# An attention kernel at its batch boundaries: two normalizing instructions moved behind two copies, and in step 2 two copies moved ahead of two weighings

## The chip, the cores and the metric

The kernel runs on one core of a Trainium2 chip. The metric is the device time of one execution in microseconds (us); lower is better. A core has a matrix engine (PE), a vector engine (DVE), a scalar engine (ACT), a general engine (POOL) and a queue engine that here only issues DMAs (SP). Each works through its own instructions in the order in which they are written; semaphores tie the engines together.

## What is computed

```
x = x + autocorrelation(layernorm(x), ctx, ctx)      # 8 batches, 512 x 2048 each, 8 heads
x = x + ffn(layernorm(x), A_w, B_w, Wq_w, keys)      # 64 experts of rank 8, 16 of them kept

autocorrelation:  corr = ifft(fft(q) * conj(fft(k))).real        # over the 512 positions
                  w, idx = top_k(corr, 12); w = softmax(w)
                  out = sum_i w_i * v[min(idx_i + pos, 511)]
ffn:              gate = softmax over the 16 best of (x Wq^T) keys^T, else 0
                  out  = ((x A^T) * gate) B^T * 2
```

Only the first line, the attention, is touched by the change.

## The kernel before

**Steps.** The attention is cut into 32 groups of 512 columns (`GROUPS`), four to a batch, and runs in 33 steps, written out one after the other. Step `i` has two halves that belong to different groups. For its own group `i` it transforms ctx and x (PE: `ctx_cyclic`, `x_spectrum`, `ctx_negacyclic`), multiplies the spectra (DVE `products`), adds the products (POOL `add_products`, tile `p_f`), goes back to lags (PE `first_corr`, `second_corr`, tile `lag`) and picks the 12 best lags with their softmax weights (DVE `topk`, ACT `big_exp`, `top_exp`, `weigh`). For the group before it, `i - 1`, it finishes the picking of the last two of four tiles, folds the weights (POOL `fold_w`, `fold_edges`), transforms them, multiplies, and turns the result back (PE `out_row`, line L755); `copy_even` (ACT, L1535) and `add_att` (DVE, L1229 and L1230) combine the two halves of that result.

**Names.** `k` is the batch of the step counted from -1, and `r` the quarter: `i = 4k + 3 + r`. A step with `r == 3` (steps 2, 6, 10, ..., 30) computes the normalizers of the next batch. The step after it has `r == 0`; the passage from one to the other is called a boundary here.

**The start of a step on PE.** `ctx_cyclic` makes four products into two PSUM banks in turn (`evac_ps[n % 2]`, line L631). The third and fourth may start only when ACT has copied the first and the second out of their bank. Then PE computes `x_spectrum(0)` (L644), the first product of `ctx_negacyclic` (L655 and L656), `x_spectrum(1)` and three more of the former. The first of the negacyclic products uses the bank of the third cyclic one:

```python
# ctx_cyclic, n = 2 and 3:     pe.wait_ge(evac_act, 6 * i + n - 1)
# ctx_negacyclic, n < 3:       pe.wait_ge(evac_act, 6 * i + 3 + n)
```

So `ctx_negacyclic`'s n = 0 needs three copies of the step done. `x_spectrum(1)` waits for `add_att` of the step before.

**The start of a step on ACT.** First two copies of the cyclic products into `v_cyc` (`evac_from`, L1525), then `last_exponentials`: two exponentials over 512 columns (L1563) and two over 12 (L1567) for group `i - 1`; then the third and the fourth copy, two negated copies (L1529), six one-column instructions (`edges`, L1547 to L1549), and from there the weighing of tiles 2 and 3 (`weigh`, L1540), which wait for DVE, and the copies of the negacyclic products (`v_neg`).

**Normalizing.** `norm` (L1395) scales and shifts a 128 x 512 tile of x, `xf`, in place, four tiles for one group. ACT does it two groups ahead, in one piece behind its `lag_copies` where `r != 3`. In a step with `r == 3` the normalizers come late, and it is done in two halves (`norm_late`): tiles 0 and 1 behind the first `big_exp`, tiles 2 and 3 at the step's end, behind `weigh` of tiles 0 and 1 and ahead of `copy_even`. POOL's `begin_fold_x` (L1775) of the following step reads all four tiles and waits for `normed`; it stands behind `fold_w` of tiles 0 and 1 (L1811 and L1812), and behind it come `middle_fold_x` (L1779), `fold_edges` (L1818, L1819), `fold_w` of tiles 2 and 3, and two `add_products` (L1804) whose `p_f` PE's `first_corr` (L698) needs.

**Step 2** is the first step that weighs tiles 0 and 1 of the group before at its own start instead of at the end of the step before; this stands between the second copy and `last_exponentials`.

Of the kernel before, what the change touches and what calls it, by code (L numbers as in the profile page):

```python
# [16 lines left out]
GROUPS = B * GPB  # L17
LT = L // P
# [115 lines left out]
def build_program(nc, x, ctx, a_w, b_w, wq_w, keys, tables, out):  # L134
# [6 lines left out]
    with ExitStack() as st:  # L141
# [27 lines left out]
        xfs, v_cyc, v_neg = [None, None], [None, None], [None, None]  # L169
# [119 lines left out]
        def is_step(i, n):  # L289
            return isinstance(i, int) and i == n  # L290


        def evac_cyc(i, n):
            return n if is_step(i, 0) else 12 * i - 4 + n

        def evac_neg(i, n):
            return 4 + n if is_step(i, 0) else 12 * i + n
# [16 lines left out]
        def prod_w(i, n):  # L314
            return 6 * i - 2 + n - (2 if is_step(i, GROUPS) else 0)
# [1074 lines left out]
        def _(act):  # L1390
            def norm(k, r, off, tiles, src=None):
                for j in tiles:
                    t = slice(j, j + 1)
                    part = xfs[(3 + r + off) % 2][:, j, :]
                    nc.scalar.activation(part, part if src is None else src[:, j, :], ACT.Identity, bias=shift[:, t], scale=rstd[:, t]).then_inc(normed, 1)  # L1395
# [122 lines left out]
            def body(k, r, a, b, f, s):  # L1518
                i = 4 * k + 3 + r
                cur, before = (r + 1) % 2, r % 2  # L1520


                def evac_from(bank, n, dst):
                    act.wait_ge(evac_ready, n + 1)
                    nc.scalar.activation(dst, evac_ps[bank][:], ACT.Copy).then_inc(evac_act, 1)  # L1525

                def minus(dst, src, n):
                    act.wait_ge(evac_act, n)
                    nc.scalar.activation(dst, src, ACT.Copy, scale=-1.0).then_inc(minus_done, 1)  # L1529
# [7 lines left out]
                def weigh(g, t):  # L1537
                    act.wait_ge(inv_done, CT * g + t + 1)
                    act.wait_ge(picked, CT * g + t + 1)
                    nc.scalar.activation(e[:, t, :], e[:, t, :], ACT.Copy, scale=inv_sum[:, t:t + 1]).then_inc(weighted, 1)  # L1540

                def edges(g, tiles):

                    for t in tiles:
                        act.wait_ge(weighted, CT * g + t + 1)
                        first, second, third, fourth = (e[:, t, n * P:n * P + 1] for n in range(4))
                        nc.scalar.activation(third, third, ACT.Identity, bias=first, scale=-1.0).then_inc(edges_done, 1)  # L1547
                        nc.scalar.activation(pick[:, t, P:P + 1], second, ACT.Identity, bias=fourth).then_inc(edges_done, 1)
                        nc.scalar.activation(pick[:, t, 3 * P:3 * P + 1], fourth, ACT.Identity, bias=second, scale=-1.0).then_inc(edges_done, 1)  # L1549
# [20 lines left out]
                if a:  # L1570
                    if b and not is_step(i, 1):
                        act.wait_ge(prod_ready, prod_w(i - 1, 3) + 1)
                    for part in range(2):
                        evac_from(part, evac_cyc(i, part), v_cyc[cur][:, part, :])
                    if is_step(i, 2):
                        for t in (0, 1):
                            weigh(i - 1, t)
                def last_exponentials():
                    for t in (2, 3):
                        big_exp(i - 1, t)  # L1580
                    for t in (2, 3):
                        top_exp(i - 1, t)
# [1 line left out]
                if b and a and not is_step(i, 1):  # L1584
                    last_exponentials()
                if a:
                    for part in range(2):
                        evac_from(part, evac_cyc(i, 2 + part), v_cyc[cur][:, 3 + part, :])
                    if is_step(i, 1):
                        last_exponentials()  # L1590
                        evac_from(0, evac_neg(i, 0), v_neg[cur][:, 0, :])
                        edges(i - 1, (0, 1))
                    for n in range(2):
                        minus(v_cyc[cur][:, 3 * n + 2, :], v_cyc[cur][:, 3 * n, :], 6 * i + 2 * n + 1)
                        if is_step(i, 1) and n == 0:
                            for t in (2, 3):
                                weigh(i - 1, t)
                    if b and not is_step(i, 1):
                        edges(i - 1, (0, 1))
# [40 lines left out]
                norm_late = i + 2 < GROUPS and r == 3  # L1640
# [23 lines left out]
                if a:  # L1664
# [4 lines left out]
                    if not is_step(i, 1):  # L1669
                        for t in (0, 1):  # L1670
                            weigh(i, t)
                if norm_late:
                    norm(k, r, 2, range(LT // 2, LT))
                if is_step(i, GROUPS - 1):
                    edges(i, (0, 1))
                    copy_even()
# [14 lines left out]
                if is_step(i, GROUPS):  # L1691
                    tile_high(0, 3)
                    tile_root(1)
            steps(body)

            def tile_step(u, k, r, a, b, f):
# [294 lines left out]
```

## Time and profile before

| | |
|---|---|
| time, median of 3 runs | 2156.32 us (2156.14 to 2157.71) |
| the profiled execution's own time | 2156.57 us |
| its span, first to last instruction | 2154.8 us |
| granted TensorE clock over the span | 1.000 |
| PE busy | 2115.7 us (98%) |
| DVE busy | 1673.8 us (78%) |
| POOL busy | 1561.3 us (72%) |
| ACT busy | 1337.5 us (62%) |

The attention takes the span up to about 1310 us, the rest is the feed-forward part. A step of the attention lasts a little over 40 us; the shares of busy time above are averages over both parts. In the rows below, a number in square brackets is the time for which the engine stood idle ahead of that row, with what ended it. A row can stand for several instructions in a run (x2, x4); its length then reaches from the first one's start to the last one's end, and for PE the ends are modelled, so that rows overlap by some 0.17 us.

### The profile page before, as it was taken

To read this page: it belongs to the slowest core of one execution; us is meant where nothing else is said; L and a number is where in the kernel's file an instruction comes from. 1 tells how busy PE (TensorE), PEld (TensorE's weight loads), DVE (VectorE), ACT (ScalarE), POOL (GpSimd) and SP (SyncE) were. 2 spreads that over 40 slices of the span, in tenths; PEclk is the share of its full clock that TensorE was granted. 3 is DMA by queue.
4 is the path that set the end of the run, shared out by engine and by line. 5 is a ranking of instruction groups with operands and counts; after the bars stand their busy time and mean duration, and the time that the engine had idled before them with its cause. 6 is when DMAs were issued, how large, how long until landed. Compare 5 with 4: busy or idle time off the path is not lost.

```text
span 2154.8 us, 29239 instructions
## 1 busy us (share of the span) xinstructions
PE 2115.7 (98%) x8920; PEld 1328.0 (62%) x8920; DVE 1673.8 (78%) x4051; ACT 1337.5 (62%) x3051; POOL 1561.3 (72%) x965
## 2 busy tenths in 40 slices
PE   5999999999999999999999999999999999999999
PEld 2455455455455455454454454888888888888887
DVE  7999999999999999999999999644444444444443
ACT  4786786786786786786765646644444455445441
POOL 6999999999999999999999988633343433333420
PEclk9999999999999999999999999999999999999999
DMA  7232333333333332333221246544545444444431
GB/s 282 97 108 103 120 111 103 120 111 103 121 109 103 121 109 103 122 109 103 103 89 64 83 168 239 171 158 166 175 164 174 159 166 165 158 166 172 164 119 59
DMA packets 110705, 287.50 MB, mean 133 GB/s; under 512 B 7168, under 2 KB 7296, under 8 KB 109568
## 3 DMA queue, kind: packets, MB, share of 16 engines
q1 hardware_dynamic: 110592, 286.19, 38.3%
q8 instruction: 47, 0.77, 0.1%
q14 instruction: 66, 0.54, 0.1%
HBM read 219.06 MB, written 67.11 MB: 133 GB/s over the span
## 4 chain that ended last, share of the span: by engine, by line
PE 82%; DVE 7%; POOL 6%; ACT 2%; issue 2%; DMA 1%; SPq 0%; DVEq 0%; ACTq 0%; POOLq 0%
PE pair L755 11%; PE pair L749 8%; PE out L581 6%; PE out L582 6%; PE out L583 6%; PE z L583 5%; PE z L582 5%; PE z L581 5%; PE pair L644 5%; PE evac L631 4%; PE evac L655 4%; PE evac L656 4%; PE lag L698 4%; PE pair L745 4%; PE tp L600 2%; POOL r_f L1804 2%
## 5 line engine op out<-in xcount | busy, mean ns | idle before, releaser
L1838 POOL TENSOR_TENSOR rows<-rows,cin 128x1024 f32<-128x1024 f32 x48 | 117.0, 2437 | 325.7 <-DMA rows<-out_dram 273.6
L755 PE MATMUL pair<-r_f,back 128*128 128x512 f32 x768 | 342.7, 597 | 0.5 <-DVE prod L1035 0.5
L1804 POOL TENSOR_TENSOR r_f<-prod 128x1024 f32<-128x1024 f32 x128 | 303.0, 2378 | 9.3 <-DVE prod L1033 7.4
L755 PEld LDWEIGHTS pair<-r_f,back 128*128 128x128 f32 x768 | 143.0, 190 | 192.7 <-issue 146.5
L749 PE MATMUL pair<-w_sb,wts 128*128 128x512 f32 x512 | 225.1, 592 | 1.4 <-ACT w_sb L1625 0.9
L1480 ACT ACTIVATE xn<-tp 128x512 f32<-128x512 f32 x94 | 55.1, 586 | 231.0 <-PE tp L600 230.9
L581 PE MATMUL z<-a_hi,xt 128*128 128x512 f32 x496 | 195.9, 395 | 0.0
L581 PE MATMUL out<-b_hi,zt_hi 128*128 128x512 f32 x492 | 194.3, 395 | 0.0
L583 PE MATMUL z<-a_hi,xt 128*128 128x512 f32 x496 | 193.4, 390 | 0.0
L582 PE MATMUL z<-a_lo,xt 128*128 128x512 f32 x496 | 193.3, 390 | 0.0
L582 PE MATMUL out<-b_lo,zt_hi 128*128 128x512 f32 x492 | 191.6, 389 | 0.0
L583 PE MATMUL out<-b_hi,zt_lo 128*128 128x512 f32 x492 | 191.5, 389 | 0.0
L1292 DVE COPY scores<-score_sums 128x64 f32<-128x64 f32 x32 | 7.2, 224 | 206.0 <-PE score_sums L830 206.0
L749 PEld LDWEIGHTS pair<-w_sb,wts 128*128 128x128 f32 x512 | 94.8, 190 | 108.9 <-issue 108.9
L1849 POOL TENSOR_TENSOR rows<-xin,rows 128x1024 f32<-128x1024 f32 x63 | 154.4, 2451 | 9.1 <-DMA xin<-in_x_dram 3.7
L1035 DVE TENSOR_TENSOR prod<-pair,v_cyc 128x1024 f32<-128x1024 f32 x128 | 155.2, 1212 | 0.0
L1804 POOL TENSOR_TENSOR p_f<-prod 128x1024 f32<-128x1024 f32 x64 | 151.6, 2370 | 3.9 <-DVE prod L1035 2.0
L631 PE MATMUL evac<-vf,fwd 128*128 128x512 f32 x248 | 120.3, 617 | 25.4 <-POOL vf L1864 21.2
L1563 ACT ACTIVATE e<-e,neg_max 128x512 f32<-128x512 f32 x128 | 88.6, 717 | 89.2 <-DVE pick L1098 89.1
L698 PEld LDWEIGHTS lag<-lags,p_f 128*128 128x128 f32 x1024 | 123.5, 192 | 20.5 <-issue 16.5
L1322 DVE SCALAR_TENSOR_TENSOR rows<-out,rows 128x512 f32<-128x512 f32 x127 | 86.9, 685 | 62.3 <-PE out L583 62.2
L698 PE MATMUL lag<-lags,p_f 128*128 128x128 f32 (+2 forms) x1024 | 129.0, 277 | 1.1 <-POOL p_f L1804 0.7
(234 smaller groups left out, 5576.8 us busy)
## 6 DMA issues: line engine op xcount, KB each, us to landing
out_dram<-att_sb SPq DMA_DIRECT2D x32, 1024.0 KB, 4.2
rows<-out_dram SPq DMA_DIRECT2D x64, 512.0 KB, 3.8
cin<-out_dram SPq DMA_DIRECT2D x63, 512.0 KB, 4.0
xin<-in_x_dram SPq DMA_DIRECT2D x63, 512.0 KB, 4.1
vf<-in_ctx_dram SPq DMA_DIRECT2D x31, 1024.0 KB, 5.1
out_dram<-rows SPq DMA_DIRECT2D x62, 512.0 KB, 2.8
xf<-in_x_dram SPq DMA_DIRECT2D x30, 1024.0 KB, 5.3
stat_in<-in_x_dram SPq DMA_DIRECT2D x27, 1024.0 KB, 5.1
```

The lines of the kernel that those rows point to most:

```text
L581: nc.tensor.matmul(out, lhs_hi, rhs_hi, start=start, stop=False)
L582: nc.tensor.matmul(out, lhs_hi, rhs_lo, start=False, stop=False)
L583: return nc.tensor.matmul(out, lhs_lo, rhs_hi, start=False, stop=stop)
L631: nc.tensor.matmul(evac_ps[n % 2][:], fwd[:, n, :], v[:, fold, :], start=True, stop=True).then_inc(evac_ready, 1)
L644: last = nc.tensor.matmul(pair_ps[:, 2 * n + part, :], fwd[:, t, :], xfs[i % 2][:, fold, :], start=True, stop=True)
L698: return nc.tensor.matmul(lag_ps[t % 2][:, cols], p_f[:, row, t * P:(t + 1) * P], lags[:, cols], start=True, stop=True)
L749: last = nc.tensor.matmul(to, wts[:, 4 * blk - 4 + 2 * part + h, :], w_sb[:, 2 - 2 * part + h, :], start=h == 0, stop=h == 1)
L755: return nc.tensor.matmul(pair_ps[:, bank, :], back[:, 3 * bank + n, :], r_f[:, row, :], start=n == 0, stop=n == 2)
L1035: op = nc.vector.tensor_tensor(slot[:, 2:4, :], s_ps, vs[:, 1:3, :], ALU.mult)
L1804: nc.gpsimd.tensor_tensor(dst, prod[:, slot, 0:2, :], prod[:, slot, 2:4, :], ALU.add).then_inc(add_done, 1)
L1838: nc.gpsimd.tensor_tensor(half, first, other, op).then_inc(c_added, 1)
L1849: nc.gpsimd.tensor_tensor(half, xin2 if second else xin[:], half, ALU.add).then_inc(x2_added, 1)
```

## The change

Two places in ACT's program are changed; no instruction is added or taken away.

- The late half of normalizing (tiles 2 and 3, two instructions) leaves the end of the steps with `r == 3`. It is issued in the step behind, after that step's first two copies of ctx and ahead of `last_exponentials`. The condition takes in steps 3, 7, 11, 15, 19, 23 and 27, which is all boundaries at which there was a late half: seven.
- In step 2 the third and fourth copy of the cyclic products are issued right behind the first two, ahead of the weighing of tiles 0 and 1 and of `last_exponentials`.

```diff
                         act.wait_ge(prod_ready, prod_w(i - 1, 3) + 1)
                     for part in range(2):
                         evac_from(part, evac_cyc(i, part), v_cyc[cur][:, part, :])
+                    if 2 < i < GROUPS - 1 and r == 0:
+                        norm(k - 1, 3, 2, range(LT // 2, LT))
                     if is_step(i, 2):
+                        for part in range(2):
+                            evac_from(part, evac_cyc(i, 2 + part), v_cyc[cur][:, 3 + part, :])
                         for t in (0, 1):
                             weigh(i - 1, t)
                 def last_exponentials():
...
                 if b and a and not is_step(i, 1):
                     last_exponentials()
                 if a:
-                    for part in range(2):
-                        evac_from(part, evac_cyc(i, 2 + part), v_cyc[cur][:, 3 + part, :])
+                    if not is_step(i, 2):
+                        for part in range(2):
+                            evac_from(part, evac_cyc(i, 2 + part), v_cyc[cur][:, 3 + part, :])
                     if is_step(i, 1):
...
                     if not is_step(i, 1):
                         for t in (0, 1):
                             weigh(i, t)
-                if norm_late:
-                    norm(k, r, 2, range(LT // 2, LT))
                 if is_step(i, GROUPS - 1):
```

On ACT, at the boundary from step 6 to step 7, the program of before holds in a row (`xf` is the tile of x, `att_sb` the result that `copy_even` starts, `v_cyc` the copies of ctx's cyclic products, `e` the exponentials):

```order
L1557 ACTIVATE e<-lag 128x256 x2
L1540 ACTIVATE e<-e,inv_sum 128x512 x2
L1395 ACTIVATE xf<-xf,shift,rstd 128x512 x2
L1535 ACTIVATE att_sb<-pair 128x1024
L1525 ACTIVATE v_cyc<-evac 128x512 x2
L1563 ACTIVATE e<-e,neg_max 128x512 x2
L1567 ACTIVATE exp_top,exp_sum<-top,neg_max 128x12 x2
L1525 ACTIVATE v_cyc<-evac 128x512 x2
```

and the changed program:

```order
L1557 ACTIVATE e<-lag 128x256 x2
L1540 ACTIVATE e<-e,inv_sum 128x512 x2
L1535 ACTIVATE att_sb<-pair 128x1024
L1525 ACTIVATE v_cyc<-evac 128x512 x2
L1395 ACTIVATE xf<-xf,shift,rstd 128x512 x2
L1563 ACTIVATE e<-e,neg_max 128x512 x2
L1567 ACTIVATE exp_top,exp_sum<-top,neg_max 128x12 x2
L1525 ACTIVATE v_cyc<-evac 128x512 x2
```

The two instructions of L1395 have moved from ahead of the first pair of copies (and of L1535) to between the first and the second pair.

On ACT, at the start of step 2, before:

```order
L1535 ACTIVATE att_sb<-pair 128x1024
L1525 ACTIVATE v_cyc<-evac 128x512 x2
L1540 ACTIVATE e<-e,inv_sum 128x512 x2
L1563 ACTIVATE e<-e,neg_max 128x512 x2
L1567 ACTIVATE exp_top,exp_sum<-top,neg_max 128x12 x2
L1525 ACTIVATE v_cyc<-evac 128x512 x2
```

and changed:

```order
L1535 ACTIVATE att_sb<-pair 128x1024
L1525 ACTIVATE v_cyc<-evac 128x512 x4
L1540 ACTIVATE e<-e,inv_sum 128x512 x2
L1563 ACTIVATE e<-e,neg_max 128x512 x2
L1567 ACTIVATE exp_top,exp_sum<-top,neg_max 128x12 x2
```

The second pair of copies has moved ahead of two weighings, two long and two short exponentials. The other engines' programs are the same in both kernels.

## Rows read from the trace of the kernel before

**Rows 1.** The page's busy time, share of the span and instructions of each engine.
```profile
PE 2115.7 (98%) x8920; PEld 1328.0 (62%) x8920; DVE 1673.8 (78%) x4051; ACT 1337.5 (62%) x3051; POOL 1561.3 (72%) x965
```

**Rows 2.** Busy us by stretch, steps 7 and 8: length, PE, PEld, DVE, ACT, POOL.
```profile
296.68:337.38 40.70, 40.17 (x129) 20.29 (x129) 39.58 (x90) 30.28 (x76) 38.89 (x27) 1.00 0.33 110
337.38:377.59 40.21, 40.21 (x130) 20.31 (x130) 39.47 (x90) 29.20 (x74) 38.91 (x27) 1.00 0.32 111
```

**Rows 3.** Waits of PE over the span: us in total, times, longest.
```profile
PE evac L631 <- ACT v_cyc L1525: 4.1, 9, 0.5
```

**Rows 4.** PE's timeline at the boundary into step 7: start, length, instruction, idle before.
```profile
296.68 1.88 PE L631 MATMUL evac<-vf,fwd 128*128 128x512 f32 x4
299.08 1.98 PE L631 MATMUL evac<-vf,fwd 128*128 128x512 f32 x4 [0.53 <-ACT v_cyc L1525]
...
302.62 1.02 PE L655 MATMUL evac<-vf,fwd 128*128 128x512 f32 x2
...
304.34 1.88 PE L644 MATMUL pair<-xf,fwd 128*128 128x512 f32 x4
```

**Rows 5.** ACT's timeline at the same boundary.
```profile
296.13 1.51 ACT L1395 ACTIVATE xf<-xf,shift,rstd 128x512 f32<-128x512 f32 x2
297.54 1.00 ACT L1535 ACTIVATE att_sb<-pair 128x1024 f32<-128x1024 f32 x1
298.45 1.07 ACT L1525 ACTIVATE v_cyc<-evac 128x512 f32<-128x512 f32 x2
299.40 1.33 ACT L1563 ACTIVATE e<-e,neg_max 128x512 f32<-128x512 f32 x2
...
301.20 1.07 ACT L1525 ACTIVATE v_cyc<-evac 128x512 f32<-128x512 f32 x2
```

**Rows 6.** ACT's timeline at the start of step 8, no boundary.
```profile
338.50 0.60 ACT L1525 ACTIVATE v_cyc<-evac 128x512 f32<-128x512 f32 x1 [0.68 <-PE evac L631]
339.30 0.60 ACT L1525 ACTIVATE v_cyc<-evac 128x512 f32<-128x512 f32 x1 [0.20 <-PE evac L631]
339.80 1.32 ACT L1563 ACTIVATE e<-e,neg_max 128x512 f32<-128x512 f32 x2
...
341.60 1.06 ACT L1525 ACTIVATE v_cyc<-evac 128x512 f32<-128x512 f32 x2
```

**Rows 7.** PE's timeline, first negacyclic product of step 8.
```profile
342.69 1.02 PE L655 MATMUL evac<-vf,fwd 128*128 128x512 f32 x2
```

**Rows 8.** POOL's timeline in step 7.
```profile
299.17 2.36 POOL L1775 TENSOR_TENSOR half_fold<-xf 128x1024 f32<-128x1024 f32 x1
...
304.50 0.21 POOL L1818 TENSOR_TENSOR pick<-pick,e 128x4 f32<-128x4 f32 x1 [0.65 <-ACT pick L1549]
...
308.10 0.21 POOL L1818 TENSOR_TENSOR pick<-pick,e 128x4 f32<-128x4 f32 x1 [0.20 <-ACT pick L1549]
...
311.07 2.37 POOL L1804 TENSOR_TENSOR p_f<-prod 128x1024 f32<-128x1024 f32 x1 [0.29 <-DVE prod L1035]
...
320.88 2.37 POOL L1804 TENSOR_TENSOR r_f<-prod 128x1024 f32<-128x1024 f32 x1 [0.29 <-DVE prod L1033]
```

**Rows 9.** PE's timeline, the first lag products of step 7 and of step 8.
```profile
312.95 1.95 PE L698 MATMUL lag<-lags,p_f 128*128 128x128 f32 x16
...
353.02 2.10 PE L698 MATMUL lag<-lags,p_f 128*128 128x128 f32 x16
```

**Rows 10.** PE's timeline in step 2.
```profile
92.88 3.86 PE L631 MATMUL evac<-vf,fwd 128*128 128x512 f32 x8
...
99.36 1.12 PE L655 MATMUL evac<-vf,fwd 128*128 128x512 f32 x2 [0.90 <-ACT v_cyc L1525]
...
104.95 1.13 PE L655 MATMUL evac<-vf,fwd 128*128 128x512 f32 x2 [0.18 <-ACT v_neg L1525]
```

**Rows 11.** ACT's and DVE's timelines in step 2.
```profile
103.69 0.72 ACT L1540 ACTIVATE e<-e,inv_sum 128x512 f32<-128x512 f32 x1 [0.69 <-DVE e L1118]
...
99.43 1.21 DVE L1230 TENSOR_TENSOR att_sb<-att_sb,pair 128x1024 f32<-128x1024 f32 x1
```

## The prediction, made before the changed kernel was run

> **What bounds the kernel now.** I read the page's busy shares first [rows 1], then the busy time of each engine step by step [rows 2], then PE's waits [rows 3], and last the timelines around one boundary [rows 4 to 9] and in step 2 [rows 10, 11]. The span's shares name PE, but they average two parts. Step by step [rows 2] a step without a boundary lasts 40.21 us and PE is busy for all of it; DVE has 39.47 and POOL 38.91 us of work in it, so both have about a microsecond to spare, and ACT eleven. The step behind a boundary lasts 40.70 us with the same work on PE. So PE sets the pace, and a stall of PE costs its full length unless PE finds a later wait already over.
>
> The only PE wait that repeats is the third cyclic product waiting for ACT's copies: 4.1 us in 9 waits [rows 3]. Seven of them are the boundaries, 0.49 to 0.53 us each; the other two (0.31 and 0.17 us, steps 0 and 4) have another place and are not touched. At the boundary into step 7, all times from the step's first product at 296.68: PE stops after two products and goes on at 2.40 with 0.53 us idle [rows 4]. The copies that it needs start at 1.77 on ACT, since the two normalizing instructions ran up to then, and `copy_even` behind them [rows 5]. Without them the copies start at 1.12 and 1.92, each as soon as PE has its product ready [rows 6].
>
> What the stall costs: the first negacyclic product starts at 5.94 in step 7 (302.62 - 296.68) and at 5.31 in step 8 (342.69 - 337.38) [rows 2, 4, 7], so 0.63 us: 0.53 idle and 0.10 for a first matmul whose weights were not loaded under another one. But the step is only 0.49 us longer. The rest comes back at the lag products: they take 2.10 us in step 8, where they wait a little for POOL's `p_f`, and 1.95 in step 7, where PE comes later and finds it ready [rows 9].
>
> **The change at a boundary: what it takes away.** Step 7 will begin on ACT as step 8 does: `copy_even` right behind the weighing, copies at 1.12 and 1.92 [rows 6]. The stall of 0.63 us ahead of the third cyclic product is gone.
>
> **What it puts in its place.** The two normalizing instructions take 1.41 us of ACT (296.13 to 297.54 [rows 5]; the row's own length is 1.51, but the next instruction starts 1.41 behind). They now stand between the second and the third copy. In step 8 ACT starts the exponentials at 2.42 and the third copy at 4.22 [rows 6]: 1.80 us for the exponentials, the same as in step 7 (299.40 to 301.20 [rows 5]), and no idle time in between. So the third copy moves to 4.22 + 1.41 = 5.63. PE may use the bank again when this copy is done. From a copy's start to PE's start the rows give 0.63 us (298.45 to 299.08 [rows 4, 5]). So the first negacyclic product starts at 6.26. PE would be there at 5.31 [rows 7]. The stall is 0.95 us, and 0.10 for the cold first matmul: 1.05 us. Against before, when this product started at 5.94 with nothing lost at its own start, PE is 6.26 + 0.10 - 5.94 = 0.42 us later behind it. The stall is not removed but moved one bank-use down the program, and is longer there.
>
> **Is it given back later in the step?** The given-back 0.15 us at the lag products is in both versions. Three others could matter.
>
> - `x_spectrum(1)`, PE's next piece but one, waits for `add_att`; DVE does that behind its own picking, not behind ACT. Before it started at 7.66 (304.34 [rows 4]), now it is reached at 8.08: no new wait, no gain.
> - ACT itself: negated copies, edges and weighing of tile 2 move by 5.63 - 4.52 = 1.11 us. The weighing of tile 3 waited 0.67 us for DVE before (as in step 2 [rows 11]), so it and the `v_neg` copy behind it move by some 0.4 us only, and PE has moved by as much. No stall there.
> - POOL: it started `begin_fold_x` at 2.49 (299.17 [rows 8]). Now the last normalizing instruction ends at 2.42 + 1.41 + 0.10 = 3.93, and POOL starts at about 4.0: 1.5 us later. Behind it POOL has waits of 0.65, 0.20, 0.29 and 0.29 us to spend [rows 8]. Following it down: the fold pair ends at 8.69 instead of 7.17; the first edges start 1.11 us later, since ACT's do, and the folding behind them too; the 0.20 of the second edges goes, which leaves 0.9 us; the 0.29 ahead of the second `p_f` goes, which leaves 0.6. So that `p_f` starts at 15.0 instead of 14.39 (311.07). PE's lag products start at 16.27 + 0.42 = 16.69 (312.95 is 16.27 [rows 9]) and need it some 0.9 us later, at 17.58; it is done at 15.0 + 2.37 = 17.4. Covered, with 0.2 us to spare. With the last 0.29 (320.88 [rows 8]) it is in step with PE and DVE again.
>
> So step 7 gets 0.42 us longer, 41.1 us in place of 40.70, and the next step starts from the same relative state. The end of step 6 is the same: `copy_even` 1.4 us earlier helps nobody, since DVE reads it only behind its picking. The seven boundaries have the same waits within 0.04 us: 7 x 0.42 = 2.9 us longer.
>
> **Step 2.** Its third and fourth copies come behind two weighings and four exponentials; PE's first negacyclic product waits 0.90 us for them [rows 10]. Moved forward, the fourth copy starts when PE has its fourth product, 96.7 (92.88 + 3.86 [rows 10]), and the stall is gone. But `x_spectrum(1)` needs `add_att`, which ends on DVE at 100.64 (99.43 + 1.21 [rows 11]), so PE goes on at about 100.8 instead of 101.2: 0.4 us left. And the third negacyclic product waits at 104.95 for the `v_neg` copy [rows 10], which stands behind the weighing of tile 3, which waits for DVE until 103.69 [rows 11]. DVE's work there depends on nothing that is moved. PE starts this product at 104.95 as before: the gain is 0, bounded by 0.1 us of the step's length either way. POOL's first folding there starts 1.1 us later, where it had over 2 us of waiting behind it.
>
> **Sum.** The profiled execution took 2156.57 us (span 2154.8): 2156.57 + 2.9 = 2159.5. The median is 0.25 lower, so I forecast 2159.2 us. Bounds of the term: 0.3 us for a boundary if PE starts sooner behind the copy than 0.63 us, 0.6 if POOL's cover of 0.2 us is just missed: 2158.4 to 2160.5.
>
> **Rivals.**
>
> *The gap closes, faster.* The repeated wait at L631 goes and PE finds the third copy early enough. This would be 7 x 0.49 = 3.4 us less, 2152.9. For it: that wait is the only one that repeats [rows 3], and in steps without the two instructions it does not exist. Against it: ACT is back to back from 2.42 to the third copy [rows 6], with 5.31 - 4.22 - 0.63 = 0.46 us to spare, and 1.41 us are put into it. The Trainium skill (Perfetto Trace Analysis, Optimization Strategy) says to take the gaps of the limiting engine, find what blocks them and make that dependency start sooner; by this rule alone the change is right and gives this time. The rows show that it looks at one gap and not at the next use of the same bank. 7 in 100.
>
> *POOL takes over, slower.* POOL has 38.9 us of work in a step of 40.2 [rows 2] and now starts 1.5 us late against 1.4 us of waits in the rows, of which those behind ACT move too. If its start behind the normalizing, or a fold that now runs beside other DVE work, costs 0.2 us more than I count, `p_f` is late for the lag products and each further tenth is PE's. With 0.4 us beyond that point the boundary costs 0.8 us and the sum is 5.7 us: 2162.0. The Trainium skill (Perfetto Trace Analysis, Identifying the Most-Contended Engine) takes weight loads, not matmuls, as the measure of PE's headroom and plain occupancy for the others. By it PE has much headroom here (20.3 of 40.2 us in weight loads [rows 2]) and DVE and POOL are the engines to watch, which makes this rival likelier; but the step's length equals PE's busy time to 0.01 us [rows 2], and that decides for me. 13 in 100.
>
> *Nothing changes.* DVE, with 39.5 us of work, sets the step's length at a boundary, or a wait later in the step swallows the 0.42 us as the one at `p_f` swallowed 0.15. Then about 2156.3. Against it: step 7 has no other PE wait left to swallow anything. 12 in 100.
>
> **How the numbers follow.** 68 in 100 for the forecast. The likeliest is 2159.2, and the range 2156.0 to 2161.2 takes in its bounds and the case of no change, and leaves out the first rival and most of the second. What a measurement of this kernel can tell from no change is about 0.2%, 4.3 us: below 2152.0 or above 2160.6. The forecast, +0.13%, lies inside, so do the third rival and most of the first. Slower by more: the POOL rival and a small tail of the forecast, 0.14. Faster by more: 0.03. The same: 0.83.
>
> **What would show it.** In the trace of the changed kernel, PE's waits at L631 for L1525 drop from 9 to 2, and 7 appear at L655 for the same copies, near 0.8 us of idle each (0.95 less the 0.16 by which a modelled end reaches over), 5.5 us in all; the one of step 2 (0.90) is gone. Boundary steps last 41.1 us and the others 40.2. POOL waits 1.4 to 1.5 us for L1395 ahead of L1775, and its waits later in the step shrink. The wait for `v_neg` in step 2 grows from 0.18 to some 0.5. I am wrong if the boundary steps are at or below 40.7, which would mean that the third copy came in time or that PE does not need it, or above 41.4, which would put POOL on the path.

## The result

The changed kernel takes 2160.7 us (median of 22 runs, 2159.05 to 2162.05) against 2156.31 us of the kernel before (22 runs on the same chips, 2156.14 to 2159.01). The ratio is 1.0017 with a 95% interval of 1.0010 to 1.0023: a small loss, 4.4 us between the medians where 2.9 was forecast. The median lies inside the forecast range of 2156.0 to 2161.2, and 0.2 us above the bounds of the forecast's own sum (2158.4 to 2160.5).

The profile after. Times within a step are again counted from its first product on PE. The profiled execution took 2162.05 us, span 2160.2. First PE's waits, in us in total, times, longest:

```profile
PE evac L655 <- ACT v_cyc L1525: 5.5, 7, 0.8
...
PE evac L655 <- ACT v_neg L1525: 0.6, 1, 0.6
PE pair L644 <- DVE att_sb L1230: 0.5, 1, 0.5
PE evac L631 <- ACT v_cyc L1525: 0.5, 2, 0.3
```

The repeated wait at L631 [rows 3] is gone from the boundaries; the two that stay are steps 0 and 4. Seven waits at L655 for the same line of ACT have come in its place, 5.5 us against the 3.6 that the seven had cost. Next the busy time of steps 7 and 8, with the same columns as [rows 2]:

```profile
299.60:340.73 41.13, 40.35 (x130) 20.16 (x129) 39.59 (x90) 30.40 (x76) 38.88 (x27) 1.00 0.32 109
340.73:380.96 40.23, 40.23 (x129) 20.31 (x129) 39.46 (x90) 29.18 (x74) 38.92 (x27) 1.00 0.32 111
```

The boundary step has grown from 40.70 to 41.13 us, the step behind it is unchanged. All seven boundaries agree: the steps that were 40.65 to 40.71 us long are 41.10 to 41.13, 3.0 us more in all, and the steps behind step 2 that are not at one of these boundaries keep their length within 0.02 us. PE's and ACT's timelines at that boundary, which answer to [rows 4] and [rows 5]:

```profile
299.60 3.75 PE L631 MATMUL evac<-vf,fwd 128*128 128x512 f32 x8
303.19 1.88 PE L644 MATMUL pair<-xf,fwd 128*128 128x512 f32 x4
305.85 1.12 PE L655 MATMUL evac<-vf,fwd 128*128 128x512 f32 x2 [0.78 <-ACT v_cyc L1525]
...
307.68 1.88 PE L644 MATMUL pair<-xf,fwd 128*128 128x512 f32 x4
```

```profile
299.06 1.01 ACT L1535 ACTIVATE att_sb<-pair 128x1024 f32<-128x1024 f32 x1
300.72 0.60 ACT L1525 ACTIVATE v_cyc<-evac 128x512 f32<-128x512 f32 x1 [0.65 <-PE evac L631]
301.52 0.60 ACT L1525 ACTIVATE v_cyc<-evac 128x512 f32<-128x512 f32 x1 [0.20 <-PE evac L631]
302.01 1.51 ACT L1395 ACTIVATE xf<-xf,shift,rstd 128x512 f32<-128x512 f32 x2
303.42 1.32 ACT L1563 ACTIVATE e<-e,neg_max 128x512 f32<-128x512 f32 x2
...
305.22 1.06 ACT L1525 ACTIVATE v_cyc<-evac 128x512 f32<-128x512 f32 x2
```

The first copies start at 1.12 and 1.92, the third at 5.62, the first negacyclic product at 6.25 and `x_spectrum(1)` at 8.08, where it had been 7.66. ACT has been idle twice, 0.65 and 0.20 us, and then works without a gap up to the copy that PE waits for. POOL's waits in the same step, which answer to [rows 8]:

```profile
303.60 2.37 POOL L1778 TENSOR_TENSOR half_fold<-xf 128x1024 f32<-128x1024 f32 x1 [1.44 <-ACT xf L1395]
...
308.51 0.21 POOL L1821 TENSOR_TENSOR pick<-pick,e 128x4 f32<-128x4 f32 x1 [0.23 <-ACT pick L1549]
...
312.18 4.68 POOL L1807 TENSOR_TENSOR p_f<-prod 128x1024 f32<-128x1024 f32 x2
...
324.21 2.38 POOL L1807 TENSOR_TENSOR r_f<-prod 128x1024 f32<-128x1024 f32 x1 [0.19 <-DVE prod L1033]
```

A new wait of 1.44 us stands ahead of the fold, and the four waits behind it that the prediction counted have shrunk from 0.65, 0.20, 0.29 and 0.29 us to 0.23, 0, 0 and 0.19. POOL has spent most of this cover and is in time for PE: no wait for `p_f` is shown at a boundary.

**Where the other 1.5 us are.** Seven boundaries of 0.42 us are 2.9. The executions of both kernels end in three clusters, that is, groups of nearly equal times. Of the kernel before 14 lie between 2156.1 and 2156.8, 5 at 2157.6 to 2157.8, 3 at 2159.0; of the changed one 9 between 2159.0 and 2159.4, 4 at 2160.7, 9 at 2161.9. The lowest of each are 2156.14 and 2159.05: 2.9 us apart, as forecast. The median of before falls into its lowest cluster, that of the changed kernel into its middle one. The mean granted clock, which was taken of every execution, sorts those of the changed kernel without an exception: 1.000 in the nine of the lowest cluster, 0.999 in the four of the middle one, 0.998 in the nine of the highest. The same holds for every later run. Where in the kernel the clock is lost is seen in the profiled execution of the changed kernel, which is one of its highest. Busy time of the engines in three stretches of step 1 there, the third number from the right being the granted clock, and then the first two of these stretches in the profiled execution of before, one of its lowest:

```profile
65.00:68.00 3.00, 2.22 (x16) 1.85 (x14) 2.08 (x4) 2.60 (x6) 3.00 (x2) 0.65 0.31 69
68.00:71.00 3.00, 3.00 (x4) 1.43 (x5) 3.00 (x6) 2.94 (x10) 3.00 (x3) 0.50 0.06 18
71.00:74.00 3.00, 3.00 (x6) 1.24 (x5) 0.49 (x1) 2.44 (x8) 2.86 (x2) 0.71 0.00 0
```

```profile
65.00:68.00 3.00, 2.06 (x17) 1.85 (x18) 2.16 (x5) 2.85 (x6) 3.00 (x2) 1.00 0.27 51
68.00:71.00 3.00, 3.00 (x8) 1.33 (x8) 3.00 (x7) 2.94 (x11) 3.00 (x2) 1.00 0.13 37
```

The clock was down to 1.2 GHz (0.50) in step 1, before either edit acts. PE's timeline shows the cost. Step 1's first product and step 2's in the changed kernel, and step 1's in the kernel before, where step 2's is at 92.88 [rows 10]:

```profile
51.80 3.80 PE L631 MATMUL evac<-att_sb,fwd 128*128 128x512 f32 x8 [0.94 <-POOL att_sb L1908]
...
95.39 3.86 PE L631 MATMUL evac<-vf,fwd 128*128 128x512 f32 x8
```

```profile
52.06 3.80 PE L631 MATMUL evac<-att_sb,fwd 128*128 128x512 f32 x8 [0.93 <-POOL att_sb L1905]
```

Step 1 lasts 43.59 us instead of 40.82, which is 2.8 us and the whole distance between the lowest and the highest cluster. Whether the change makes this likelier, or the share is chance, is the subject of the last three runs.

### The profile page after: what moved, and what is told of

Its sections match the earlier page's. It is cut to its first block, busy times and chain, and to the rows that moved or that the text cites. A ratio compares the mean times of both kernels' runs of the same rounds, so it can differ in the third digit from the quotient of the medians.

```text
span 2160.2 us, 29239 instructions
## 1 busy us (share of the span) xinstructions
PE 2118.9 (98%) x8920; PEld 1328.2 (61%) x8920; DVE 1675.5 (78%) x4051; ACT 1338.1 (62%) x3051; POOL 1561.1 (72%) x965
## 4 chain that ended last, share of the span: by engine, by line
PE 91%; DVE 3%; ACT 2%; POOL 2%; issue 1%; DMA 1%; SPq 0%; DVEq 0%; ACTq 0%; POOLq 0%
PE pair L755 14%; PE pair L749 10%; PE out L581 6%; PE out L582 6%; PE out L583 6%; PE z L583 5%; PE z L582 5%; PE z L581 5%; PE lag L698 5%; PE evac L655 5%; PE evac L656 5%; PE pair L745 5%; PE evac L631 4%; PE pair L644 4%; PE tp L600 2%; PE score_sums L613 1%
## 5 line engine op out<-in xcount | busy, mean ns | idle before, releaser
L749 PE MATMUL pair<-w_sb,wts 128*128 128x512 f32 x512 | 227.5, 598 | 1.2 <-ACT w_sb L1630 0.8
L749 PEld LDWEIGHTS pair<-w_sb,wts 128*128 128x128 f32 x512 | 95.8, 192 | 110.4 <-issue 110.4
L631 PE MATMUL evac<-vf,fwd 128*128 128x512 f32 x248 | 118.5, 613 | 21.5 <-POOL vf L1867 21.0
L655 PE MATMUL evac<-vf,fwd 128*128 128x512 f32 x248 | 127.8, 597 | 6.0 <-ACT v_cyc L1525 5.5
```

Source lines behind the costliest of these rows:

```text
L631: nc.tensor.matmul(evac_ps[n % 2][:], fwd[:, n, :], v[:, fold, :], start=True, stop=True).then_inc(evac_ready, 1)
L655: nc.tensor.matmul(evac_ps[n % 2][:], fwd[:, t, :], v[:, first, :], start=True, stop=False)
L749: last = nc.tensor.matmul(to, wts[:, 4 * blk - 4 + 2 * part + h, :], w_sb[:, 2 - 2 * part + h, :], start=h == 0, stop=h == 1)
```

## The experiments

Times are compared by cluster where clusters exist: "lowest" is the median of the lowest one. The ratios with their 95% intervals are of all executions to those of the kernel before on the same chip, and so hold the clusters' share as well. On the chip of the first four runs the kernel before has it at 2156.87 (18 of 33 executions).

### The boundary part alone

```diff
                     for part in range(2):
                         evac_from(part, evac_cyc(i, part), v_cyc[cur][:, part, :])
+                    if 2 < i < GROUPS - 1 and r == 0:
+                        norm(k - 1, 3, 2, range(LT // 2, LT))
...
-                if norm_late:
-                    norm(k, r, 2, range(LT // 2, LT))
```

> The boundary part alone: the two normalizing instructions behind the first two copies, step 2 as before. My account (two instructions of 1.41 us put between the second and the third copy, PE 0.42 us later at each of seven boundaries): boundary steps 41.12 us long, PE waits 5.5 us at L655 for L1525 in seven pieces plus the 0.90 of step 2, 2.9 us more than before when the first 100 us run at the same granted clock. Rival (part of the 4.4 us comes from step 2's reordering): this kernel is about 1.5 us faster than the full change, while the other 1.5 us appear in the kernel with step 2 alone.

Measured: 2159.55 us (11 executions, 8 of them in the lowest cluster around 2159.54), 2.7 us above the lowest of before, where 2.9 was expected; ratio 1.0008 (0.9999 to 1.0017). The busy time of step 7:

```profile
296.91:338.03 41.12, 40.34 (x129) 20.17 (x129) 39.60 (x90) 30.39 (x76) 38.86 (x27) 1.00 0.31 109
```

and PE's wait:

```profile
PE evac L655 <- ACT v_cyc L1525: 6.4, 8, 0.9
```

The whole loss is in this part. The wait is 5.5 us of the boundaries and 0.9 of step 2. The rival, that this kernel would be 1.5 us faster than the full change, has fallen.

### Step 2's part alone

```diff
                     if is_step(i, 2):
+                        for part in range(2):
+                            evac_from(part, evac_cyc(i, 2 + part), v_cyc[cur][:, 3 + part, :])
                         for t in (0, 1):
                             weigh(i - 1, t)
...
-                    for part in range(2):
-                        evac_from(part, evac_cyc(i, 2 + part), v_cyc[cur][:, 3 + part, :])
+                    if not is_step(i, 2):
+                        for part in range(2):
+                            evac_from(part, evac_cyc(i, 2 + part), v_cyc[cur][:, 3 + part, :])
```

> Step 2's part alone: all four copies ahead of weighing, normalizing as before. My account: 0, that is step 2 as long as before within 0.1 us and the time that of before within 0.2 us at the same granted clock; PE's wait at L655 for L1525 (0.90) is gone, in its place 0.5 us at L644 for DVE's att_sb and 0.55 instead of 0.18 for v_neg. Rival (step 2's part costs the 1.5 us that my forecast lacks): 1.5 us more than before in every execution, and a step 2 that is longer by as much. A third possibility: the granted clock falls between 65 and 74 us in some executions of any of these kernels, and then 1.4 or 2.8 us are added whatever the edit.

Measured: 2156.91 us, ratio 0.9997 (0.9988 to 1.0006); lowest cluster 2156.91 against 2156.87. PE's timeline in step 2, which answers to [rows 10]:

```profile
92.67 3.85 PE L631 MATMUL evac<-vf,fwd 128*128 128x512 f32 x8
96.36 1.88 PE L644 MATMUL pair<-xf,fwd 128*128 128x512 f32 x4
98.07 1.02 PE L655 MATMUL evac<-vf,fwd 128*128 128x512 f32 x2
...
100.47 1.98 PE L644 MATMUL pair<-xf,fwd 128*128 128x512 f32 x4 [0.52 <-DVE att_sb L1230]
...
104.73 1.12 PE L655 MATMUL evac<-vf,fwd 128*128 128x512 f32 x2 [0.56 <-ACT v_neg L1525]
```

The wait of 0.90 us is gone and its time has been cut into two others, 0.52 for DVE and 0.56 in place of 0.18 for the `v_neg` copy. The third negacyclic product starts 12.06 us into the step, before it was 12.07, and the step is 42.15 us long instead of 42.18. The gain is nothing that can be told.

### The late half in an idle stretch of ACT

If the price comes from what stands in ACT's queue, the two instructions should cost nothing where ACT is idle anyway. In step 6 of the kernel before ACT waited 1.74 us for DVE between the two pairs of copies of `lag_copies((2, 3))`:

```profile
294.30 0.71 ACT L1557 ACTIVATE e<-lag 128x256 f32<-128x256 f32 x2 [1.74 <-DVE lag L1067]
```

```diff
-                def lag_copies(tiles):
+                def lag_copies(tiles, between=None):
...
                         nc.scalar.activation(e[:, t, 0:2 * P], lag_ps[t % 2][:, 0:2 * P], ACT.Copy).then_inc(cos_copied, 1)
+                    if between:
+                        between()
...
-                    lag_copies((2, 3))
+                    lag_copies((2, 3), (lambda: norm(k, r, 2, range(LT // 2, LT))) if norm_late else None)
...
-                if norm_late:
-                    norm(k, r, 2, range(LT // 2, LT))
```

> The late half of normalizing between ACT's two pairs of lag copies of tiles 2 and 3, in the same step (L1554 and L1557), where ACT stood idle for 1.74 us in step 6 and the two instructions take 1.41. My account (the price is set by what stands in ACT's queue ahead of the next copy that PE needs, so idle time of ACT takes it for nothing): no wait of PE at L631 or L655 at the seven boundaries, boundary steps 40.2 us, POOL's begin_fold_x as early as before, 7 x 0.49 = 3.4 us less than before: 2152.9. Rival (DVE or POOL would hold the boundary step anyway): boundary steps stay at 40.7 us with PE waiting for DVE or POOL, and the time that of before.

Measured: 2155.19 us (11 executions; 5 in the lowest cluster around 2153.6, 5 in the highest, among them the profiled one), ratio 0.9988 (0.9979 to 0.9997). Lowest against lowest it is 3.3 us less; 3.4 was expected. ACT's timeline at the end of step 6 and the start of step 7:

```profile
294.06 0.62 ACT L1554 ACTIVATE e<-lag 128x256 f32<-128x256 f32 x2
294.59 1.51 ACT L1395 ACTIVATE xf<-xf,shift,rstd 128x512 f32<-128x512 f32 x2
296.42 0.71 ACT L1559 ACTIVATE e<-lag 128x256 f32<-128x256 f32 x2 [0.32 <-DVE lag L1067]
297.03 1.33 ACT L1540 ACTIVATE e<-e,inv_sum 128x512 f32<-128x512 f32 x2
298.26 1.01 ACT L1535 ACTIVATE att_sb<-pair 128x1024 f32<-128x1024 f32 x1
299.87 0.60 ACT L1525 ACTIVATE v_cyc<-evac 128x512 f32<-128x512 f32 x1 [0.60 <-PE evac L631]
```

The wait for DVE is 0.32 us where it was 1.74: the two instructions took its place. Step 7:

```profile
298.76:339.07 40.31, 40.31 (x129) 20.25 (x129) 39.48 (x90) 29.27 (x74) 38.96 (x27) 1.00 0.33 111
```

No PE wait for ACT is left at a boundary, and the step is 40.31 us long, 0.1 above a step without a boundary. So the time of the prediction's first rival, the gap closing, can be had; it depends on where the two instructions go and not on whether they leave.

### One of the two instructions

```diff
+                    if 2 < i < GROUPS - 1 and r == 0:
+                        norm(k - 1, 3, 2, (3,))
...
                 if norm_late:
-                    norm(k, r, 2, range(LT // 2, LT))
+                    norm(k, r, 2, (2,))
```

> Half a dose: tile 2 is normalized at the end of the step as before, tile 3 behind the next step's first two copies. My account: one instruction of 0.705 us ends in time for the first copy (copy_even at 0.16, first copy still at 1.12 us), so no wait at L631; the other puts the third copy at 4.22 + 0.705 = 4.93 and PE at 5.56 instead of 5.31, a wait of 0.25 and 0.10 for the cold matmul. Boundary steps 40.4 to 40.6 us, 7 x (-0.15 to -0.35) = 1 to 2.4 us less than before, and 4 to 5.3 less than the full change at equal clock. Rival (it is POOL's later start, not the third copy, that costs): POOL starts 0.75 us later than before, so the boundary step is longer than before and lies halfway between 40.70 and 41.12.

Measured: 2154.83 us, lowest cluster 2154.63 (6 of 11), 2.2 less than before's lowest; ratio 0.9989 (0.9980 to 0.9998). PE's timeline at the boundary and the busy time of step 7:

```profile
296.22 3.75 PE L631 MATMUL evac<-vf,fwd 128*128 128x512 f32 x8
299.81 1.88 PE L644 MATMUL pair<-xf,fwd 128*128 128x512 f32 x4
301.78 1.13 PE L655 MATMUL evac<-vf,fwd 128*128 128x512 f32 x2
```

```profile
296.22:336.65 40.43, 40.34 (x129) 20.16 (x129) 39.54 (x90) 30.54 (x76) 38.89 (x27) 1.00 0.32 111
```

The first negacyclic product starts at 5.56, as computed, 0.25 us later than without a wait (5.31). The modelled end of the row before hides most of this, and the 0.09 us that are left get no bracket. Two instructions in this place cost 0.42 us against before, one gains 0.27. A price in proportion to how much was moved would have to lie between before and the change; this one is below both. What sets it is how late each copy comes for the moment at which PE needs its bank.

### Both behind the fourth copy

The copies are then all in time, and POOL's fold is later still.

```diff
                         evac_from(part, evac_cyc(i, 2 + part), v_cyc[cur][:, 3 + part, :])
+                    if 2 < i < GROUPS - 1 and r == 0:
+                        norm(k - 1, 3, 2, range(LT // 2, LT))
...
-                if norm_late:
-                    norm(k, r, 2, range(LT // 2, LT))
```

> Both normalizing instructions behind the next step's fourth copy, so that no copy that PE waits for stands behind them. If only ACT's queue ahead of the copies set the price, the boundary steps would be 40.2 us long and the time 3.4 us less than before. My account has POOL's cover too: begin_fold_x would start at 6.8 us of the step instead of 2.5, which is far more than POOL's waits of 1.4 us, so POOL reaches the end of its folding at about 14.9 (PE wants to turn the weights at 13.9) and the second p_f at 19.5 (PE wants it at 16.5). Boundary steps 42.5 to 43.5 us, PE waiting for POOL at L692 and L698, 7 x 2 to 2.8 = 14 to 20 us more than before. Rival: POOL catches up in between by having its products earlier, boundary steps below 41.5.

Measured: 2173.48 us (4 executions), 17.3 us above the lowest cluster of before on the chip of this run and the next three (2156.2); ratio 1.0081 (1.0066 to 1.0097). POOL's and PE's timelines in step 7, which begins at 298.86:

```profile
305.62 2.36 POOL L1775 TENSOR_TENSOR half_fold<-xf 128x1024 f32<-128x1024 f32 x1 [4.22 <-ACT xf L1395]
...
313.63 4.67 POOL L1804 TENSOR_TENSOR p_f<-prod 128x1024 f32<-128x1024 f32 x2
```

```profile
313.73 0.66 PE L692 MATMUL evac<-ident,pick 128*128 128x128 f32 x4 [0.57 <-POOL pick L1819]
...
316.04 1.16 PE L698 MATMUL lag<-lags,p_f 128*128 128x128 f32 x8 [0.35 <-POOL p_f L1804]
318.36 1.16 PE L698 MATMUL lag<-lags,p_f 128*128 128x128 f32 x8 [1.15 <-POOL p_f L1804]
```

POOL waits 4.22 us, more than its later waits can make up, and PE waits three times for it. The step is 43.13 us long. So the second rival, POOL on the path, exists; it needs a later fold than the change makes.

### Keeping PE busy in step 1

In all kernels so far PE stood idle for 2.1 us in step 1, from about 62.7 to 64.8 us. Two matmuls whose result is overwritten later are put there, in the changed kernel, in the one before, and in the one with normalizing between the lag copies:

```diff
+                def wait_in_one():
+                    pe.wait_ge(prod_ready, prod_x(1, 0) + 1)
+                    for _ in range(2):
+                        nc.tensor.matmul(pair_ps[:, 0, :], fwd[:, 0, :], fwd[:, 0:4, :].rearrange("p n m -> p (n m)"), start=True, stop=True)
...
                     ctx_negacyclic((0, 1, 2, 3))
+                    wait_in_one()
```

> The changed kernel with two matmuls whose result nobody reads, in step 1 behind the negacyclic products, where PE stood idle from 62.7 to 64.8 us before it turned weights. Executions of all kernels so far end in three clusters 1.4 us apart; in the two profiled executions of the highest cluster the granted clock was 0.50 (1.2 GHz) in the stretch 68 to 71 us, right behind this idle time, and the first weights products took 2.4 us longer. My account: with PE busy there the clock stays at 1.00 and nearly all executions lie in the lowest cluster, 2159.5 us here. Rival (the clock falls for another reason, or the clusters come from elsewhere): the three clusters stay, with a third to two thirds of the executions above the lowest.

> The same two matmuls in the kernel before. My account: all executions at 2156.8 us, the lowest cluster of the kernel before on this chip, and with the run above a difference of 2.7 to 2.9 us that no clock disturbs. Rival: the three clusters of before stay. If the two matmuls delay PE (they end at about 64.9, when PE goes on), up to 0.1 us more.

> The late half of normalizing between ACT's lag copies, and the two matmuls in step 1. My account: all executions at 2153.6 us, the lowest cluster of the kernel with normalizing in that place: 3.3 us below the lowest cluster of before and some 4 us below its mean. Rival as in the two runs above: the clusters stay and the median is somewhere between 2153.5 and 2156.5.

Measured, 11 executions each:

| kernel | median | all executions | ratio to before |
|---|---|---|---|
| changed, PE busy | 2159.35 us | 2159.09 to 2159.69 | 1.0010 (1.0001 to 1.0019) |
| before, PE busy | 2156.27 us | 2156.10 to 2156.96 | 0.9998 (0.9989 to 1.0007) |
| between the lag copies, PE busy | 2153.20 us | 2153.05 to 2153.77 | 0.9981 (0.9972 to 0.9990) |
| before, same chip | 2157.51 us | 2156.15 to 2159.51 | |

The clusters are gone in all three kernels: 33 executions of 33 have a granted clock of 1.000 and are in what was the lowest one, while the kernel before beside them had 12 of 27 there. The times are up to 0.5 us below the expected ones, which went by the first chip; the differences to the kernel before with PE busy are 3.1 us up, where 2.7 to 2.9 was expected, and 3.1 us down, where 3.3 was. The first stretches of step 1 in the changed kernel with PE busy:

```profile
62.00:65.00 3.00, 2.81 (x10) 1.23 (x10) 3.00 (x4) 2.97 (x9) 3.00 (x6) 1.00 0.00 0
65.00:68.00 3.00, 2.06 (x15) 1.61 (x14) 2.17 (x4) 2.85 (x7) 3.00 (x2) 1.00 0.24 84
```

and of the changed kernel without them the first stretch, and the single microsecond behind 66:

```profile
62.00:65.00 3.00, 0.90 (x5) 0.37 (x4) 3.00 (x4) 2.97 (x10) 3.00 (x6) 1.00 0.00 0
66.00:67.00 1.00, 1.00 (x6) 0.76 (x4) 0.55 (x1) 0.95 (x2) 1.00 (x2) 0.50 0.18 31
```

PE was busy for 0.90 us of the three ahead of the fall, and is for 2.81 now. In the profiled execution of before it was busy for 0.89 of them, and its clock stayed at 1.00: the idle stretch makes the fall possible and does not bring it every time. Without the clock's part the changed kernel is 3.1 us slower than before.

Nor do the counts show that the change makes the fall likelier: without the added matmuls the kernel before had 44 of 82 executions in its lowest cluster, the changed kernel 9 of 22, and the changed kernel and the five variants together 39 of 70. The 1.5 us by which the median exceeded the forecast come from the cluster that the middle one of the 22 executions happened to fall into.

The last kernel beats both: 3.1 us below the kernel before with PE busy, and 4.3 us below the median of before beside it, of which the added matmuls account for 1.2. Its step 7, 40.24 us long, is within 0.03 of a step without a boundary:

```profile
295.97:336.21 40.24, 40.24 (x129) 20.36 (x129) 39.48 (x90) 29.20 (x74) 38.94 (x27) 1.00 0.32 111
```

## Why the prediction was right

**PE sets the pace.** In every variant the boundary step, 40.24 to 43.13 us long, became longer or shorter as PE's waits did, while the work of DVE in it, 39.5 to 39.7 us, and of POOL, 38.7 to 39.0 us, hardly changed.

**What the change takes away.** As forecast: the copies at 1.12 and 1.92, no wait shown at L631. The 0.63 us of the stall were right as a sum, but not their parts, 0.53 idle and 0.10 for a slower first matmul. Without the stall, too, the eight cyclic products take 3.59 us (299.60 to 303.19), where eight at the 0.43 us of the rows around them are 3.43: the third is slower in both cases and waits a little even here. The stall is wait alone, partly hidden by the modelled end of the row before.

**What it puts in its place.** Forecast the third copy at 5.63, PE at 6.26, `x_spectrum(1)` at 8.08; measured 5.62, 6.25 and 8.08. The idle time shown was to be near 0.8 us in seven pieces, 5.5 in all; it is 0.78 and 5.5. The boundary step was to last 41.1 us; it lasts 41.13. The run with one instruction (5.56, as computed) and the one in ACT's idle stretch show the same cause from two other sides.

**POOL's cover.** Forecast: the fold at about 4.0, the first edges 1.11 us later (at 8.93), the second `p_f` done at 17.4 with 0.2 us to spare. Measured 4.00, 8.91 and 17.26, and no wait of PE for `p_f`. That the cover is finite, and roughly as large as counted, is shown by the run behind the fourth copy: 43.13 us where 42.5 to 43.5 was expected.

**Step 2.** Forecast 0, with at most 0.1 us of the step's length either way; measured 0.03 us of the step's length and 0.04 us between the lowest clusters. Both barriers behind the removed wait, `att_sb` and `v_neg`, appear as named.

**The sum.** The term is 2.9 us: 2.9 between the fastest executions, 2.7 with the boundary part alone, 3.1 with PE kept busy. The forecast of 2159.2 is the changed kernel's lowest cluster. The median came out at 2160.7, since the forecast took the distance between cluster and median to be the same in both kernels. The kernel before already showed one of its three runs at 2157.71, 1.4 to 1.6 us above the other two, and I read over it. So it was luck that the range held the median: the bounds of the sum ended at 2160.5, and the range reached further for other reasons. The prediction also gave 0.83 to a difference too small to tell, up to 2160.6; the median is just beyond that, and the interval leaves out a ratio of 1. The mechanism and the size of its term are right, and the clock's part was missing.

**The rivals.** The gap did not close: the third copy had 0.46 us to spare, and 1.41 us were put ahead of it. The rule of the Trainium skill (Perfetto Trace Analysis, Optimization Strategy), to make the dependency behind a gap start sooner, is right about the gap; the trace differs from what it gives by itself here, +2.9 us instead of -3.4, because ACT owes PE a second copy close behind the first ones. POOL did not take over, though it did with a later fold, in the run behind the fourth copy. The Trainium skill (Perfetto Trace Analysis, Identifying the Most-Contended Engine) judges PE's headroom by its weight loads, among other things. They fill half of a step here (20.16 of 41.13 us), and by that PE looks half idle; the runs side with PE's waits. *Nothing changes* fell too: all seven boundary steps grew by 0.41 to 0.45 us, and no later wait swallowed it.

## What to carry to other kernels

Before an instruction is moved out of the way of one waiting engine, list every later thing in the same queue that anyone waits for, with the time by which it is due; the place for it is where its own engine is idle for longer than it takes (here 1.74 us idle for 1.41 us of work), and not merely behind the wait that is seen. A stall that goes is worth only what the next dependency leaves of it: here 0.63 us taken away and 1.05 put in, and in step 2 0.9 taken away and nothing gained. And where a few microseconds matter, look at all executions and not at the median alone.

## What the hardware showed that was not expected

Behind a wait of PE of 2.1 us early in the kernel the granted clock fell from 2.4 to 1.2 GHz in something under half of the executions (69 of the 152 without the added matmuls, by their times), and in none of the 33 in which the wait was filled. In both profiled executions of a highest cluster it was below 1.00 in the stretches from 65 to 74 us. In that of the changed kernel sixteen matmul records of the weights took 9.47 us, and in the kernel before 7.11:

```profile
64.66 0.63 PE L692 MATMUL evac<-ident,pick 128*128 128x128 f32 x4 [2.10 <-ACT v_neg L1525]
...
67.94 9.47 PE L749 MATMUL pair<-w_sb,wts 128*128 128x512 f32 x16 [0.78 <-ACT w_sb L1630]
```

```profile
67.81 7.11 PE L749 MATMUL pair<-w_sb,wts 128*128 128x512 f32 x16 [0.94 <-ACT w_sb L1625]
```

The shorter wait ahead of L749 did not bring the fall: the clock was at 0.50 a microsecond earlier, in the stretch from 66 to 67 us in which PE was busy throughout, and with the longer wait filled a wait of 0.94 us stays there and the clock holds.

The price is 2.8 us between the lowest and the highest cluster. The middle cluster, at half of this, has a mean clock of 0.999, between the 1.000 and the 0.998 of the others; that fits a fall half as long, but none of its executions was profiled, so its place and length stay open. Later waits in the attention, 0.5 to 1.2 us each in otherwise busy stretches, left the clock at 1.00 in every row read.
